# Rotary halves swapped by DMA, softmax row sums on ScalarE, and a reordered start of self-attention in a gated cross-attention and mixture-of-experts layer

## The chip, the cores and the metric

One core of a Trainium2 chip runs the whole layer in one launch. The metric is the device time in microseconds of one execution. Lower is better.

## The reference, cut to what matters

Eight sequences of 100 rows by 512 go through gated cross-attention (16 heads of 128 over 361 context rows), and the result, normalised, goes through a block with its own causal self-attention (16 heads of 32, rotary positions) and a mixture of experts. The change touches the self-attention and what feeds it:

```python
h = _rms(x, w_ln1)                       # x: the layer-normed rows after cross-attention
q, k, v = h @ wq + bq, h @ wk + bk, h @ wv + bv    # 16 heads of 32
def rot(t):
    t1, t2 = (t[..., :D // 2], t[..., D // 2:])
    return jnp.concatenate([-t2, t1], axis=-1)
q, k = q * cos + rot(q) * sin, k * cos + rot(k) * sin
scores = jnp.einsum('bqhd,bkhd->bhqk', q, k) * HEAD_DIM ** (-0.5)   # causal mask, then
attn = jax.nn.softmax(scores, axis=-1)
ctx = jnp.einsum('bhqk,bkhd->bqhd', attn, v)
```

## The kernel before, in words

**Engines and order.** Five programs, one for each of SyncE (SP, the loads of weights), ScalarE (ACT), VectorE (DVE), GpSimd (POOL) and TensorE (PE), walk the same list of steps. The list of this part is `steps_ffn` (L216 to L300). Each engine does its share of a step in the order of the list and waits on semaphores in that order; nothing is taken out of turn.

**Precision.** Most products are three matmuls of rounded high and low parts. ScalarE makes the high part, DVE (activations, L1290) or POOL (weights, L1827) subtracts it to get the low part. A weight tile costs an SP load (L731) into one of four `raw` buffers, a ScalarE copy (L846) and a POOL subtraction. Weights are loaded six units and split four units ahead of the matmuls that use them.

**Halves.** The eight sequences are two halves of four. While PE does the last projection of cross-attention, the first half is already normalised and transposed to `HTh`/`HTl`. For each sequence b of the second half the chain is: `resid` b (PE transposes `YT`; DVE adds it to `XR` and takes the statistics, L1441 and L1442), `norm1` b (DVE, `Z`), `square` b (ScalarE root), `row` b (DVE, into `HR`), `turn` b (PE transposes, ScalarE writes `HTh`, DVE `HTl`). Before the change all of it stands between `vrow` 0 and `qk` (0,1): PSUM banks 6 and 7 serve `resid`, banks 4 and 5 serve `turn`, which are free until the first softmax tile is transposed. `vrow` k (four of them) are the value projection, 12 matmuls each; its bias add (four DVE instructions, L1485) stands in `vrow` 3.

**Query and key tiles.** There are 16, (h, n) with h the half and n from 0 to 7; n even is a query tile, n odd the key tile of the same four heads. `qk` (h, n) is 12 matmuls of 400 columns into bank 6 or 7, then ScalarE writes `PQ[..][:, 0, :]` with bias (L1044). There are two `PQ` buffers; ScalarE waits that the tile two before is done. `rope` (h, n) is on DVE a shuffle of the halves of each head into `PQ[..][:, 1, :]` (L1472), a product with `sinT` (L1474) and, once POOL's product with `cosT` (L1889) is there, the sum (L1477). In the second part of the list `rope` stands right behind the `at` step beside which its tile was made.

**Self-attention.** `at` n, for n from 0 to 35, is one pipeline step; score tile u (one head of each of four sequences, 100 rows by 4 x 100) is taken through it:

- every fourth step PE makes the scores of four tiles (mask by matmul, then 16 small products; `f_scores`), after the exponentials of the four tiles before;
- in step u: DVE takes the row minimum (`f_max`, L1497), ScalarE the exponential, four instructions of 100 columns (L1066);
- in step u + 1: DVE sums the rows of the exponentials (L1519) and inverts the sum (L1520), POOL multiplies (L1897);
- in step u + 3: PE transposes (L2264), ScalarE or DVE (L1507) copies to `PTf`;
- every fourth step, `f_out`: PE multiplies with the values into bank 4, ScalarE writes `CXh`, DVE `CXl`. Bank 4 is also one of the two for transposed tiles, so the next odd tile's transposition waits for `CXl`.

Beside the steps stand matmuls that PE can do meanwhile: `qk` (0,4) to (0,7) at 0, 1, 3, 4, the values of the second half (`vbat`) at 6 to 9, `qk` (1,0) to (1,5) at 10, 11, 13, 15, 17, 18, the output projection `po` of half 0 at 20 to 23, `qk` (1,6) and (1,7) at 24 and 25, and from 24 on the epilogue of half 0 (`er`: residual and statistics on DVE; `eroot`, `erms`, `eh`: norm and transposition; router).

**Banks.** `banks` in the class `Plan` deals banks 6 and 7 alternately to the steps that use them, in the order of the list, and notes which semaphore says that the last user is done.

Of the kernel before, what the change touches and what calls it, by code (L numbers as in the profile page):

```python
# [43 lines left out]
ROUTE = {"order": 2, ("sg", 0): 5, "picks": 6, ("sg", 1): 8, "pad": 10, "eid": 11, "pos": 12, "idx": 13, "mine": 14}  # L44
SWAP = [(i + 16) % 32 for i in range(32)]

# [169 lines left out]
def steps_ffn():  # L216
# [21 lines left out]
    yield from vrow(0) + [("resid", 4), ("norm1", 4)]
    yield from vrow(1) + [("square", 4), ("row", 4), ("resid", 5), ("norm1", 5)]
    yield from vrow(2) + [("square", 5), ("row", 5), ("resid", 6), ("norm1", 6), ("turn", 4)]  # L240
    yield from vrow(3) + [("square", 6), ("row", 6), ("resid", 7), ("norm1", 7), ("turn", 5)]
    yield from qk(0, 0) + [("square", 7), ("row", 7), ("rope", 0, 0), ("turn", 6)]
    yield from qk(0, 1) + [("rope", 0, 1), ("turn", 7)]
    yield from qk(0, 2) + [("rope", 0, 2)]
    yield from qk(0, 3) + [("rope", 0, 3), ("router_split",)]
# [80 lines left out]
class Plan:  # L326
# [86 lines left out]
    def banks(self):  # L413

        empty = {6: ("dve_x1", 7), 7: ("dve_x1", 8)}
        self.bank, self.bank_free = {}, {}
# [13 lines left out]
        for s in self.ffn:  # L430
            if s[0] == "qk":
                use(s, ("act_f", s[1] * 8 + s[2] + 1))
# [45 lines left out]
def flamingo_kernel(nc, x, ctx_in, mask, g_x, g_f, Wq, Wk, Wv, Wo, w_ln1, wq, b_q, wk, b_k, wv, b_v, wo,  # L478
# [242 lines left out]
    def sync_program(eng):  # L721
# [62 lines left out]
        def zero_rows():  # L784
# [46 lines left out]
    def scalar_program(eng):  # L831
# [191 lines left out]
        def turn(b):  # L1023
            act.wait_ge(sem("pe_ht"), b + 1)
            src = banks[4 + b % 2][:, 0:KD * T].rearrange("p (k t) -> p k t", k=KD)
            eng.activation(HTh[b // HB][:, :, batch_slice(b)], src, ACT.Copy).then_inc(sem("act_ht"), 1)
# [20 lines left out]
        def self_attention(n):  # L1047
# [227 lines left out]
    def vector_program(eng):  # L1275
# [157 lines left out]
        def resid(b):  # L1433
# [4 lines left out]
            dve.wait_ge(sem("pool_const"), CONST["causal"])  # L1438
            stt(XR[:, i, :], banks[6 + i % 2][0:T, :], tgx[:, 0:1], XR[:, i, :], ALU.mult, ALU.add).then_inc(sem("dve_x1"), 1)
            dve.wait_ge(sem("dve_x1"), b + 1)  # L1440
# [21 lines left out]
        def turn(b):  # L1462
            dve.wait_ge(sem("act_ht"), b + 1)
            src = banks[4 + b % 2][:, 0:KD * T].rearrange("p (k t) -> p k t", k=KD)
# [14 lines left out]
        def v_row(k):  # L1479
            if k < KD - 1:  # L1480
                return
            for i in range(HB):
# [16 lines left out]
        def self_attention(n):  # L1499
# [245 lines left out]
        for name, *a in plan.ffn:  # L1745
# [12 lines left out]
            elif name == "rope":  # L1758
                rope(*a)
            elif name == "vrow":  # L1760
                v_row(*a)
            elif name == "vadd":
# [208 lines left out]
    def tensor_program(eng):  # L1971
# [178 lines left out]
        def resid(b):  # L2150
            half, i = divmod(b, HB)
            pe.wait_ge(sem("act_yt"), KD * (half + 1))
            if i >= 2:
                pe.wait_ge(sem("dve_x1"), b - 1)
            elif i == 0:
                pe.wait_ge(sem("dve_pt"), 2 * NS * (half + 1))
            else:
                pe.wait_ge(sem("dve_o"), NS * (half + 1))
            for f in range(KD):
                e = eng.transpose(banks[6 + i % 2][0:T, f * 128:(f + 1) * 128], YT[:, f, i * T:(i + 1) * T], ident[:, :])  # L2160
            e.then_inc(sem("pe_rows"), 1)

        def turn(b):
            if b >= 2:
                pe.wait_ge(sem("dve_ht"), b - 1)
            elif b == 0:
                pe.wait_ge(sem("dve_j"), plan.job_end[1])
            else:
                pe.wait_ge(sem("dve_pt"), 4 * NS)
            pe.wait_ge(sem("dve_row"), b + 1)  # L2170
            for k in range(KD):
                e = eng.transpose(banks[4 + b % 2][:, k * T:(k + 1) * T], HR[b % 3][:, k * 128:(k + 1) * 128], ident[0:T, 0:T])
            e.then_inc(sem("pe_ht"), 1)
# [39 lines left out]
        def f_scores(q):  # L2213
# [19 lines left out]
        def f_out(q):  # L2233
# [5 lines left out]
            if q:  # L2239
                pe.wait_ge(sem("dve_cx"), q)  # L2240
            else:
                pe.wait_ge(sem("dve_ht"), B - 1)
            for b in range(HB):
# [279 lines left out]
```

## Time and profile before

| | |
|---|---|
| runs, median of 3 | 1006.71 us (1005.0 to 1008.25) |
| profiled execution, its own time | 1002.62 us |
| its span, first to last instruction | 1000.8 us |
| mean granted TensorE clock | 0.949 |
| PE busy / DVE / ACT / POOL | 90% / 67% / 55% / 42% |

The profiled execution is 4.1 us (0.4%) below the median. The profile records every instruction with its start and length in us from the span's start; "[4.03 <-POOL PF L1897]" behind a record is the idle time of its engine ahead of it and what ended it. Matmuls are pipelined, so the length of one is more than the distance to the next. `vrow` 0 starts at 471.8 us and the last step of self-attention ends at about 655 us; the change lies wholly in between.

### The profile page before, as it was taken

The page shows a single profiled execution, that of the slowest core. Times are in us where ns is not written, and L with a number is a line of the kernel's source. Part 1 is how long each engine was busy: PE and PEld are TensorE (multiplying, and loading weights), DVE is VectorE, ACT ScalarE, POOL GpSimd, SP SyncE. Part 2 cuts the span into 40 slices and gives each one's busy share as a digit, 9 for nine tenths or more (in the row PEclk, how much of TensorE's full clock was granted, in tenths as well). Part 3 has the DMA queues.
Part 4 walks back from the last instruction along what each step waited for, and adds up shares of the span by engine and source line. Part 5 has one row for each costly group of instructions (what it writes and reads, how often), then busy time and mean ns, then how long its engine had stood idle before and what let it go on. Part 6 is the DMA issues. An engine that isn't in the chain of part 4 may idle for free.

```text
span 1000.8 us, 16056 instructions
## 1 busy us (share of the span) xinstructions
PE 903.5 (90%) x5713; PEld 838.3 (84%) x5713; DVE 666.5 (67%) x1492; ACT 555.3 (55%) x1305; POOL 422.0 (42%) x405
## 2 busy tenths in 40 slices
PE   4999999999999999999887884899887989999995
PEld 4889999999989999998676774698877988898884
DVE  4557777753747776732887758656855878897853
ACT  3656666744556666644345452435435667776750
POOL 3442322345532322346376552254272545565531
PEclk9999999999999999999989796599998999999998
DMA  5763000035520000035222120033478799999975
GB/s 141 207 229 91 1 1 2 11 98 151 155 68 16 2 1 1 12 85 142 86 64 64 38 60 21 1 97 94 161 220 218 220 292 285 295 307 292 275 181 143
DMA packets 125687, 120.75 MB, mean 121 GB/s; under 512 B 12644, under 2 KB 96556, under 8 KB 125008
## 3 DMA queue, kind: packets, MB, share of 16 engines
q1 hardware_dynamic: 106510, 96.09, 31.3%
q0 software_dynamic: 5120, 10.22, 5.1%
q10 hardware_dynamic: 13978, 13.41, 4.8%
q8 instruction: 46, 0.75, 0.3%
q14 instruction: 33, 0.27, 0.1%
HBM read 102.16 MB, written 17.53 MB: 120 GB/s over the span
## 4 chain that ended last, share of the span: by engine, by line
PE 58%; DVE 15%; DMA 13%; ACT 5%; issue 5%; POOL 4%; ACTq 0%; SPq 0%; POOLq 0%; DVEq 0%
PE bank L1976 52%; DMA eraw<-in_L_ffn_w_down_e_dram 4%; PE bank L2103 3%; DVE we L1290 2%; DMA s_sum<-yo,target 2%; POOL s_rows L1904 2%; DVE PQ L1474 1%; DMA eraw<-in_L_ffn_w_gate_e_dram 1%; ACT we L860 1%; DMA eraw<-in_L_ffn_w_up_e_dram 1%; DMA s_rows<-HR,idx 1%; DMA raw<-in_L_xattn_Wq_dram 1%; DMA sums<-s_sum 1%; DVE wf L1290 1%; DVE PQ L1472 1%
## 5 line engine op out<-in xcount | busy, mean ns | idle before, releaser
L1856 POOL TENSOR_SCALAR SC<-SC,mx,anyv 100x361 f32<-100x361 f32 x128 | 81.5, 647 | 211.3 <-DVE mx L1403 200.9
L1839 POOL TENSOR_TENSOR we<-eraw,we 128x704 fp32r<-128x704 f32 x40 | 72.7, 1818 | 112.0 <-ACT we L860 110.3
L1827 POOL TENSOR_TENSOR wx<-raw,wx 128x512 fp32r<-128x512 f32 x64 | 83.5, 1313 | 80.4 <-ACT wx L846 80.3
L860 ACT ACTIVATE we<-eraw 128x704 fp32r<-128x704 f32 (+2 forms) x140 | 96.6, 718 | 29.6 <-DMA eraw<-in_L_ffn_w_down_e_dram 16.5
L1290 DVE TENSOR_TENSOR we<-eraw,we 128x704 fp32r<-128x704 f32 (+2 forms) x100 | 92.8, 946 | 24.4 <-ACT we L860 24.1
L1976 PE MATMUL bank<-H2h,wf 128*128 128x400 f32 x352 | 102.1, 357 | 0.0
L1827 POOL TENSOR_TENSOR wf<-raw,wf 128x512 fp32r<-128x512 f32 x54 | 70.9, 1317 | 60.5 <-ACT wf L846 60.2
L975 ACT ACTIVATE SC<-SC,mx 100x361 f32<-100x361 f32 x128 | 75.4, 593 | 27.7 <-DVE mx L1399 27.1
L1976 PE MATMUL bank<-XTh,wx 128*128 128x400 f32 x256 | 72.7, 357 | 2.8 <-POOL wx L1827 1.4
L1290 DVE TENSOR_TENSOR Kl<-bank,Kh 128x362 fp32r<-128x362 f32 x64 | 34.2, 535 | 60.2 <-ACT Kh L933 60.2
L846 ACT ACTIVATE wf<-raw 128x512 fp32r<-128x512 f32 x100 | 61.8, 629 | 19.3 <-DMA raw<-in_L_ffn_w_sh_down_dram 7.6
L1290 DVE TENSOR_TENSOR QOl<-bank,QOh 128x200 fp32r<-128x200 f32 (+1 forms) x96 | 41.5, 432 | 44.4 <-ACT QOh L889 34.3
L1976 PE MATMUL bank<-QOh,wx 128*128 128x400 f32 x256 | 70.5, 347 | 0.0
L1976 PEld LDWEIGHTS bank<-H2h,wf 128*128 128x128 f32 x352 | 67.7, 194 | 0.3 <-issue 0.2
L1396 DVE CUSTOM_DVE_ANT_0 SC<-bank,mb 100x361 f32<-100x361 f32 x128 | 62.7, 528 | 0.3
L1976 PE MATMUL bank<-H2l,wf 128*128 128x400 f32 x176 | 62.0, 353 | 0.0
L966 ACT ACTIVATE PTh<-bank 128x400 fp32r<-128x400 f32 x64 | 32.3, 505 | 50.1 <-PE bank L2103 50.0
L1290 DVE TENSOR_TENSOR wf<-raw,wf 128x512 fp32r<-128x512 f32 x46 | 48.0, 1051 | 17.5 <-ACT wf L846 17.0
L1290 DVE TENSOR_TENSOR PTl<-bank,PTh 128x400 fp32r<-128x400 f32 (+1 forms) x128 | 53.3, 459 | 7.5 <-ACT PTh L966 7.5
L1066 ACT ACTIVATE PF<-bank,sm 100x100 f32<-100x100 f32 x128 | 33.7, 355 | 44.2 <-DVE sm L1497 44.2
L1897 POOL TENSOR_TENSOR PF<-PF,sm 100x400 f32<-100x400 f32 x32 | 27.9, 873 | 69.1 <-DVE sm L1520 69.1
L846 ACT ACTIVATE wx<-raw 128x512 fp32r<-128x512 f32 x64 | 40.0, 627 | 30.5 <-PE bank L1976 12.2
(265 smaller groups left out, 2824.8 us busy)
## 6 DMA issues: line engine op xcount, KB each, us to landing
eraw<-in_L_ffn_w_gate_e_dram SPq DMA_DIRECT2D x40, 352.0 KB, 3.9
eraw<-in_L_ffn_w_up_e_dram SPq DMA_DIRECT2D x40, 352.0 KB, 5.6
eraw<-in_L_ffn_w_down_e_dram SPq DMA_DIRECT2D x40, 256.0 KB, 6.3
raw<-in_L_xattn_Wq_dram SPq DMA_DIRECT2D x32, 256.0 KB, 3.1
raw<-in_L_xattn_Wo_dram SPq DMA_DIRECT2D x32, 256.0 KB, 3.0
raw<-in_L_ffn_w_sh_gate_dram SPq DMA_DIRECT2D x22, 256.0 KB, 3.4
raw<-in_L_ffn_w_sh_up_dram SPq DMA_DIRECT2D x22, 256.0 KB, 3.3
s_rows<-Z SPq DMA_DIRECT2D x6, 800.0 KB
```

The lines of the kernel that those rows point to most:

```text
L846: eng.activation(weights(stream, u)[:, 0, :, :], raw[r % 4][:, :, :], ACT.Copy).then_inc(sem("act_w"), 1)
L860: eng.activation(weights("e", u)[0:rows, 0, 0:n], eraw[u % 6][0:rows, 0:n], ACT.Copy).then_inc(sem("act_e"), 1)
L966: eng.activation(flat(PTh[t % 2][:, 0:2, :]), banks[5][:, 0:4 * T], ACT.Copy).then_inc(sem("act_pt"), 1)
L975: eng.activation(sc, sc, ACT.Exp, bias=mx[t % 3][:, 1, h:h + 1], scale=XS, accum_out=mx[t % 3][:, 2, h:h + 1]).then_inc(sem("act_exp"), 1)
L1066: e = eng.activation(p[:, c, :], bank[0:T, c * T:(c + 1) * T], ACT.Exp, bias=m[:, 1, c:c + 1], scale=-1.0)
L1290: return eng.tensor_tensor(o, src, f32(hi), ALU.subtract)
L1396: eng.tensor_tensor_reduce(SC[t % 3][:, h, :], banks[h][0:T, 0:S], mb[:, :], 1.0, -3.0e38, ALU.add, ALU.max, m[:, 0, h:h + 1]).then_inc(se ...
L1827: eng.tensor_tensor(w[:, 1, :, :], raw[plan.raw[stream, u] % 4][:, :, :], f32(w[:, 0, :, :]), ALU.subtract).then_inc(sem("pool_w"), 1)
L1839: eng.tensor_tensor(w[0:rows, 1, 0:n], eraw[u % 6][0:rows, 0:n], f32(w[0:rows, 0, 0:n]), ALU.subtract).then_inc(sem("pool_e"), 1)
L1856: eng.tensor_scalar(sc, sc, m[:, 3, h:h + 1], anyv[:, b:b + 1], ALU.mult, ALU.mult).then_inc(sem("pool_p"), 1)
L1976: return eng.matmul(o, a, b, start=start, stop=stop, skip_group_check=True)
L2103: e = eng.transpose(dst, SC[t % 3][:, h, o:o + n], ident[0:T, 0:T])
```

## The change

- **Sums**: the exponential on ScalarE also gives the sum of its row (`accum_out`); the DVE reduction L1519 goes.
- **Swap**: the shuffle L1472 goes. SP waits for `PQ[..][:, 0, :]` and issues eight DMAs of 16 partitions by 400 elements (25.6 KB each) that write each half of a head's rows to the place of the other; DVE waits for all eight. They stand in SP's program where `rope` stands in the list.
- **Order**: `norm1`, `square`, `row`, `turn` are spread later; the bias add of the values becomes a step (`vout`) ahead of `turn` 4; `qk` (0,3) goes behind the first scores, so that three tiles instead of five are made before them; each later tile of half 0 moves by one to two steps.
- **Banks**: `resid` and `turn` of the second half take banks 6 and 7 from the same deal as the `qk` tiles. First scores and first transpositions wait for `turn` 3 only.

```diff
+    yield from vrow(0) + [("resid", 4)]
+    yield from vrow(1) + [("resid", 5), ("norm1", 4), ("square", 4)]
+    yield from vrow(2) + [("resid", 6), ("row", 4), ("norm1", 5), ("square", 5)]
+    yield from vrow(3) + [("row", 5), ("vout",), ("turn", 4)]
+    yield from qk(0, 0) + [("norm1", 6), ("square", 6), ("rope", 0, 0), ("turn", 5)]
+    yield from qk(0, 1) + [("row", 6), ("rope", 0, 1), ("resid", 7), ("router_split",)]
+    yield from qk(0, 2)
...
-    beside = {0: qk(0, 4), 1: qk(0, 5), 3: qk(0, 6), 4: qk(0, 7), 6: v[0], 7: v[1], 8: v[2], 9: v[3],
+    beside = {0: [("rope", 0, 2), ("turn", 6)], 1: qk(0, 3) + [("norm1", 7), ("square", 7)], 2: [("row", 7)] + qk(0, 4),
+              3: qk(0, 5) + [("turn", 7)], 4: qk(0, 6), 5: qk(0, 7), 6: v[0], 7: v[1], 8: v[2], 9: v[3],
...
-        empty = {6: ("dve_x1", 7), 7: ("dve_x1", 8)}
+        empty = {6: ("dve_pt", 4 * NS), 7: ("dve_o", 2 * NS)}
...
+            if s[0] == "resid" and s[1] >= HB:
+                use(s, ("dve_x1", s[1] + 1))
+            elif s[0] == "turn" and s[1] >= HB:
+                use(s, ("dve_ht", s[1] + 1))
...
+        def rotate(h, n):
+            at = 8 * h + n
+            p = PQ[at % 2]
+            sp.wait_ge(sem("act_f"), at + 1)
+            for q in range(8):
+                a, b = 16 * q, 16 * (q ^ 1)
+                eng.dma_start(p[a:a + 16, 1, :], p[b:b + 16, 0, :]).then_inc(sem(f"dma_rot{at % 2}"), 16)
...
                     e = eng.activation(p[:, c, :], bank[0:T, c * T:(c + 1) * T], ACT.Exp, bias=m[:, 1, c:c + 1],
-                                       scale=-1.0)
+                                       scale=-1.0, accum_out=m[:, 2, c:c + 1])
...
         def rope(h, n):
-            dve.wait_ge(sem("act_f"), at + 1)
-            chained(eng.stream_shuffle(p[:, 1, :], p[:, 0, :], SWAP))
+            dve.wait_ge(sem(f"dma_rot{at % 2}"), 128 * (at // 2 + 1))
...
                 dve.wait_ge(sem("act_fe"), u + 1)
-                chained(eng.tensor_reduce(m[:, 2, :], PF[u % 4][:, :, :], AX, ALU.add))
                 eng.reciprocal(m[:, 3, :], m[:, 2, :]).then_inc(sem("dve_fr"), 1)
...
         def f_scores(q):
-                pe.wait_ge(sem("dve_ht"), B)
+                pe.wait_ge(sem("dve_ht"), HB)
```

## Rows read from the trace of the kernel before

**Rows 1.** Busy time by stretch: window, length, then busy (count) of each engine
```profile
core 0: us, PE busy (x) PEld busy (x) DVE busy (x) ACT busy (x) POOL busy (x), PEclk, DMA share, GB/s
471.00:505.00 34.00, 29.23 (x140) 24.18 (x140) 25.43 (x51) 12.03 (x26) 16.84 (x27) 0.90 0.35 99
...
523.00:545.00 22.00, 20.34 (x173) 15.48 (x166) 17.70 (x37) 11.20 (x37) 11.81 (x13) 1.00 0.13 39
545.00:582.00 37.00, 24.89 (x257) 21.34 (x255) 28.78 (x56) 17.70 (x55) 22.40 (x22) 0.82 0.19 58
...
600.00:622.00 22.00, 8.70 (x69) 7.91 (x68) 17.79 (x37) 6.24 (x17) 6.53 (x7) 0.72 0.08 24
```

**Rows 2.** Waits, 545 to 583 us: total, times, longest
```profile
ACT PF L1066 <- DVE sm L1497: 16.5, 6, 4.3
...
PE bank L2264 <- DVE CXl L1290: 7.0, 2, 4.8
```

**Rows 3.** The chain that ended last, 471 to 655 us, by line
```profile
by line: PE bank L1976 31.8%; DVE PQ L1474 8.0%; issue 7.9%; DVE PQ L1472 3.6%; PE bank L2264 3.3%; DVE sm L1497 3.2%; POOL wf L1827 2.9%; ACT PF L1066 2.7%; DVE HR L1287 2.6%; DVE sm L1519 2.1%; DVE KT L1477 2.1%; POOL PF L1897 2.0%; DVE Q
```

**Rows 4.** The two DVE operations that go, and the product behind the shuffle: ns min/median/max
```profile
L1472 DVE STREAM_SHUFFLE PQ<-PQ x16: 593/602/619, 497.6 to 612.2; 128x400 f32<-128x400 f32 x16
L1474 DVE TENSOR_TENSOR PQ<-PQ,sinT x16: 574/1362/3009, 498.2 to 612.9; 128x400 f32<-128x400 f32 x16
...
L1519 DVE TENSOR_REDUCE sm<-PF x32: 555/559/571, 513.7 to 646.7; 100x4 f32<-100x400 f32 x32
```

**Rows 5.** Exponentials of cross-attention, which have a sum: timeline, ScalarE
```profile
201.32 0.60 ACT L975 ACTIVATE SC<-SC,mx 100x361 f32<-100x361 f32 x1
...
201.81 0.20 ACT L975 ACTIVATION_READ_ACCUMULATOR SC<-SC,mx 100x1 f32 x1
201.90 0.59 ACT L975 ACTIVATE SC<-SC,mx 100x361 f32<-100x361 f32 x1
```

**Rows 6.** Small transfers issued back to back on ScalarE's queue: timeline
```profile
24.60 0.36 ACTq L894 DMA_DIRECT2D mask<-in_mask_BxS_bf_dram  x1
24.99 0.36 ACTq L895 DMA_DIRECT2D Z<-in_c_causal_dram  x1
```

**Rows 7.** DMA issues, 455 to 620 us: count, KB each, median us to landing
```profile
raw<-in_L_ffn_wv_dram SPq DMA_DIRECT2D x6, 256.0 KB, 2.6
...
WR<-in_L_ffn_w_sh_eg_dram ACTq DMA_DIRECT2D x1, 2.0 KB, 3.3
```

**Rows 8.** The same chain in order of time: start, us, what
```profile
451.43 6.58 PE bank L1976 x36
```

**Rows 9.** TensorE at the first scores, first transposition, second scores: timeline
```profile
505.13 0.85 PE L1976 MATMUL bank<-causb,identb 100*100 100x400 bf16 x4 [0.22 <-DVE HTl L1290]
...
515.48 0.91 PE L2264 MATMUL bank<-ident,PF 100*100 100x100 f32 x4 [4.03 <-POOL PF L1897]
...
521.51 0.85 PE L1976 MATMUL bank<-causb,identb 100*100 100x400 bf16 x4 [0.47 <-ACT PF L1066]
```

**Rows 10.** Fourth scores to fifth scores, around tile (1,2): timeline
```profile
552.44 1.54 PE L1976 MATMUL bank<-causb,identb 100*100 100x400 bf16 x4
...
559.30 0.60 ACT L1044 ACTIVATE PQ<-bank,bqn 128x400 f32<-128x400 f32 x1 [1.46 <-PE bank L1976]
...
562.46 0.56 DVE L1507 COPY PTf<-bank 100x400 f32<-100x400 f32 x1
563.08 0.89 PE L1976 MATMUL bank<-PTf,V 100*32 100x100 f32 x32 [0.56 <-DVE PTf L1507]
565.45 0.57 DVE L1290 TENSOR_TENSOR CXl<-bank,CXh 128x400 fp32r<-128x400 f32 x1 [1.27 <-ACT CXh L1058]
566.84 1.54 PE L1976 MATMUL bank<-causb,identb 100*100 100x400 bf16 x4
```

**Rows 11.** Tiles (1,6) and (1,7) on DVE: timeline
```profile
602.85 3.01 DVE L1474 TENSOR_TENSOR PQ<-PQ,sinT 128x400 f32<-128x400 f32 x1
...
612.22 0.60 DVE L1472 STREAM_SHUFFLE PQ<-PQ 128x400 f32<-128x400 f32 x1
```

More of the change, by code:

```diff
@@ L44 @@
 ROUTE = {"order": 2, ("sg", 0): 5, "picks": 6, ("sg", 1): 8, "pad": 10, "eid": 11, "pos": 12, "idx": 13, "mine": 14}
-SWAP = [(i + 16) % 32 for i in range(32)]
 WO_AT = (NS - 6, NS, NS + 1, NS + 2)
@@ L236, in qk @@
         return [fetch, ("qk", h, n)]
[L238 to L245, printed above, removed]
+    yield from vrow(0) + [("resid", 4)]
[5 more added lines that the diff above has]
+    yield from qk(0, 2)
     v = [[("vbat", 0), fetch], [("vadd", 0), ("vbat", 1), fetch], [("vadd", 1), ("vbat", 2)], [("vadd", 2), ("vbat", 3)]]
     po = [[[fetch, ("po", h, m)] for m in range(KD)] for h in range(2)]
-    beside = {0: qk(0, 4), 1: qk(0, 5), 3: qk(0, 6), 4: qk(0, 7), 6: v[0], 7: v[1], 8: v[2], 9: v[3],
+    beside = {0: [("rope", 0, 2), ("turn", 6)], 1: qk(0, 3) + [("norm1", 7), ("square", 7)], 2: [("row", 7)] + qk(0, 4),
+              3: qk(0, 5) + [("turn", 7)], 4: qk(0, 6), 5: qk(0, 7), 6: v[0], 7: v[1], 8: v[2], 9: v[3],
               10: [("vadd", 3), fetch, fetch] + qk(1, 0), 11: qk(1, 1), 13: qk(1, 2), 15: qk(1, 3), 17: qk(1, 4),
@@ L430, in banks @@
         for s in self.ffn:
-            if s[0] == "qk":
+            if s[0] == "resid" and s[1] >= HB:
+                use(s, ("dve_x1", s[1] + 1))
+            elif s[0] == "turn" and s[1] >= HB:
+                use(s, ("dve_ht", s[1] + 1))
+            elif s[0] == "qk":
                 use(s, ("act_f", s[1] * 8 + s[2] + 1))
@@ L816, in sync_program @@
                 asked["f"] += 1
+            elif name == "rope":
+                rotate(*a)
             elif name == "fetch_e":
@@ L1024, in turn @@
             act.wait_ge(sem("pe_ht"), b + 1)
-            src = banks[4 + b % 2][:, 0:KD * T].rearrange("p (k t) -> p k t", k=KD)
+            src = banks[plan.bank["turn", b] if b >= HB else 4 + b % 2][:, 0:KD * T].rearrange("p (k t) -> p k t", k=KD)
             eng.activation(HTh[b // HB][:, :, batch_slice(b)], src, ACT.Copy).then_inc(sem("act_ht"), 1)
@@ L1438, in resid @@
             dve.wait_ge(sem("pool_const"), CONST["causal"])
-            stt(XR[:, i, :], banks[6 + i % 2][0:T, :], tgx[:, 0:1], XR[:, i, :], ALU.mult, ALU.add).then_inc(sem("dve_x1"), 1)
+            bank = banks[plan.bank["resid", b] if b >= HB else 6 + i % 2]
+            stt(XR[:, i, :], bank[0:T, :], tgx[:, 0:1], XR[:, i, :], ALU.mult, ALU.add).then_inc(sem("dve_x1"), 1)
             dve.wait_ge(sem("dve_x1"), b + 1)
@@ L1463, in turn @@
             dve.wait_ge(sem("act_ht"), b + 1)
-            src = banks[4 + b % 2][:, 0:KD * T].rearrange("p (k t) -> p k t", k=KD)
+            src = banks[plan.bank["turn", b] if b >= HB else 4 + b % 2][:, 0:KD * T].rearrange("p (k t) -> p k t", k=KD)
             at = batch_slice(b)
@@ L1479, in v_row @@
         def v_row(k):
-            if k < KD - 1:
-                return
             for i in range(HB):
@@ L1759, in vector_program @@
                 rope(*a)
-            elif name == "vrow":
-                v_row(*a)
+            elif name == "vout":
+                v_row(KD - 1)
             elif name == "vadd":
@@ L2152, in resid @@
             pe.wait_ge(sem("act_yt"), KD * (half + 1))
[L2153 to L2156, printed above, removed]
-            else:
-                pe.wait_ge(sem("dve_o"), NS * (half + 1))
+            if half:
+                bank = free_bank(("resid", b))
+            else:
+                bank = banks[6 + i % 2]
+                if i >= 2:
+                    pe.wait_ge(sem("dve_x1"), b - 1)
+                elif i == 0:
+                    pe.wait_ge(sem("dve_pt"), 2 * NS)
+                else:
+                    pe.wait_ge(sem("dve_o"), NS)
             for f in range(KD):
-                e = eng.transpose(banks[6 + i % 2][0:T, f * 128:(f + 1) * 128], YT[:, f, i * T:(i + 1) * T], ident[:, :])
+                e = eng.transpose(bank[0:T, f * 128:(f + 1) * 128], YT[:, f, i * T:(i + 1) * T], ident[:, :])
             e.then_inc(sem("pe_rows"), 1)
         def turn(b):
[L2164 to L2167, printed above, removed]
-            else:
-                pe.wait_ge(sem("dve_pt"), 4 * NS)
+            if b >= HB:
+                bank = free_bank(("turn", b))
+            else:
+                bank = banks[4 + b % 2]
+                if b >= 2:
+                    pe.wait_ge(sem("dve_ht"), b - 1)
+                elif b == 0:
+                    pe.wait_ge(sem("dve_j"), plan.job_end[1])
+                else:
+                    pe.wait_ge(sem("dve_pt"), 4 * NS)
             pe.wait_ge(sem("dve_row"), b + 1)
             for k in range(KD):
-                e = eng.transpose(banks[4 + b % 2][:, k * T:(k + 1) * T], HR[b % 3][:, k * 128:(k + 1) * 128], ident[0:T, 0:T])
+                e = eng.transpose(bank[:, k * T:(k + 1) * T], HR[b % 3][:, k * 128:(k + 1) * 128], ident[0:T, 0:T])
             e.then_inc(sem("pe_ht"), 1)
@@ L2240, in f_out @@
                 pe.wait_ge(sem("dve_cx"), q)
-            else:
-                pe.wait_ge(sem("dve_ht"), B - 1)
             for b in range(HB):
@@ L2255, in self_attention @@
                     pe.wait_ge(sem("dve_v"), HB)
-                    pe.wait_ge(sem("dve_ht"), B - 1)
+                    pe.wait_ge(sem("dve_ht"), HB)
                 elif u % 2 == 0:
```

## The prediction

> **What bounds the kernel now.** I first cut the stretch of the change, 471 to 655 us, into stages by busy time [rows 1]. Up to 505 PE has 29.2 of 34 us; from 523 to 545 it has 20.3 of 22 and is the bound. From 545 to 582 it has only 24.9 of 37 at a granted clock of 0.82, while DVE has 28.8: the softmax pipeline and the tiles (1,0) to (1,5) keep DVE late, and PE waits. From 600 to 622 PE has 8.7 of 22 and DVE 17.8 (tiles (1,6), (1,7), epilogue). The waits of 545 to 583 say how [rows 2]: ScalarE waited 16.5 us for row minima, PE 7.0 us for `CXl`, both from DVE. The chain that ended last [rows 3] holds, besides matmuls (31.8% of 184 us), the sin product with 8.0%, the shuffle with 3.6% (6.6 us) and the row sum with 2.1% (3.9 us). So what counts is not DVE's total but when DVE gets through its queue, in order: a wait in it costs as much as work.
>
> **The change, part by part.**
>
> *Row sums.* Gone from DVE: 32 x 0.56 = 17.9 us busy, about 0.5 each in the pipeline [rows 4]. Added on ScalarE: one accumulator read per instruction. In cross-attention the read starts 0.49 after its exponential and the next exponential 0.09 after the read [rows 5]; so 4 x 0.09 = 0.4 us more per step, 12 us in all, on an engine busy 17.7 of 37 us in the tightest stage [rows 1]. From exponential to reciprocal the way is equal (+0.4, and -0.5 for the reduction); from exponentials to the next scores it is 0.4 longer, once in four steps. Bounds for the read: 0.09 (added distance) and 0.20 (its own length) each; I take 0.09, as four stand in a row.
>
> *Swap.* Gone: 16 shuffles of 0.60 [rows 4]. In their place, for each tile: SP waits for `PQ`, issues eight DMAs, DVE waits for the last. The distance of two issues is 0.39 [rows 6], so the eighth is issued 7 x 0.39 = 2.7 us after the first; SP spends 3.1 us a tile, 50 in all. The landing of 25 KB within SBUF is nowhere in the trace. The nearest rows are 2.6 us for 256 KB and 3.3 for 2 KB, both out of HBM [rows 7]; that the smaller is not the faster says size is not the price. Above I allow 3.3; below, 0.4 (one issue and nothing). I take 2.3, a little under the nearest row, as 25 KB is a tenth of it. Together **5.0 us** from `PQ` to sin product (3.1 to 6.0), against 0.6. So +4.4 us per tile wherever DVE stands ready and something hangs on what is queued behind `rope`: the next row minimum, then exponential, then scores; the copies to `PTf`; `CXl`.
>
> The Trainium skill, SBUF — State Buffer, section "Can I just issue two DMAs to hit both halves?", says that two transfers at different partitions serialize; this is taken up under the rivals. The skill's DMA: Bandwidth & Descriptors, section Anatomy of one DMA, puts the fixed price of a transfer at about 2.0 us (for GpSimd's path); an estimate with it is 4.7 us a tile and a total some 1.5 us lower.
>
> *POOL against DVE.* The sin product has min 0.57, median 1.36, max 3.0 us for one shape [rows 4]; it is long where POOL works beside it (3.01 at 602.85 [rows 11]). After the change it starts some 4 us later, when POOL's cosine product of the tile is over, and I take 0.57 to 0.9: this gives back about 0.8 a tile.
>
> *Start (471 to 523).* One tile is 12 matmuls at 6.58/36 = 0.18 us, 2.2 us [rows 8]. DVE order is now row 5, value bias, `turn` 4, norm 6, rope (0,0), `turn` 5. Stepping through: `vrow` 3 ends at 486, value bias at 490.9, `turn` 4 low part 491.5, so bank 7 is free for `turn` 5 only then (PE idle 2.3). rope (0,0) is fed at 495.1 and done at 497, `turn` 5 low part 497.6: `resid` 7 waits for that bank (idle 3). rope (0,1) is fed at about 500.8, `resid` 7 on DVE 503.3, `turn` 6 on PE 503.4 (idle 2 to 3), first scores 503.9. Before they were at 505.1 [rows 9], with five tiles made; now three. rope (0,2) stands ahead of the first minimum: fed at 506.8, minimum at 509.5. The idle of 4.0 us ahead of the first transposition at 515.5 [rows 9] is filled by (0,3) to (0,5). The second scores come at 521.6 against 521.5 [rows 9], but (0,7) is still to be made: **+2.0** (0 to +5).
>
> *523 to 545.* PE-bound; DVE has slack for (0,6) and (0,7), and PE's waits there are under 2 us: **0**. If the cover goes (DVE late by a rotation at 528 and 532, ahead of `f_out` 0) it costs up to 2.
>
> *545 to 582.* Three links. (a) Ahead of the fourth scores DVE already waited 3 us for POOL at tile (1,0); rotation (1,0) is fed at 549.6, so most is covered: +1.2, and +0.5 for the accumulating exponential: +1.7. (b) Fourth to fifth scores took 14.4 us [rows 10]. The chain is `PQ` written at 559.9, shuffle and products, copy to `PTf` 562.5, `f_out` 563.1, `CXl` 565.4, scores 566.8 [rows 10]. The shuffle's 0.6 becomes 5.0; exponential +0.4; less stretching -0.3; sums not on this stretch: +4.2 (rounded down for PE's overlap). (c) Fifth scores to `po`: tile (1,4) +4.1, but (1,5) is landed by the time DVE gets there: -0.6 for its shuffle, -0.8 for its product: +2.7. Sum **+8.6**.
>
> *582 to 600.* `po` keeps PE busy, no tiles: **0**.
>
> *600 to 655.* Tile (1,6): `PQ` at 599.7, fed at 604.7, done 605.9, against 606.4 (the 3.01 goes [rows 11]): -0.5. Tile (1,7): DVE waited for `PQ` [rows 11], so +4.4 - 0.3, ahead of the statistics and root of the epilogue. Behind it three sums on the chain, -1.5, and one exponential, +0.5: **+2.6**.
>
> **Sum:** 2.0 + 0 + 8.6 + 0 + 2.6 = +13.2 us. Against the profiled execution 1002.6 + 13.2 = 1015.8. That execution is 4.1 under the median, so the median would be 1019.9; I say **1019.5**, as the hand-stepping takes no slack twice. SP's loads are hidden: it loads six units ahead, and a tile's rotation holds it until 3.1 us after `PQ`; without this cover each dense tile costs about 2 us.
>
> **Rivals.**
>
> (A) *Relief wins.* If a landing is short and DVE comes late anyway, the chain loses shuffle and sum, 6.6 + 3.9 us [rows 3], keeps +1.5 for the reads: -9, 998. For it: DVE is the busiest engine in two stages [rows 1]. Against: at (1,2) DVE had waited for `PQ`, so the new wait is bare. It decides where `PQ` to product is under about 1.5 us; the eight issues alone are 2.7. Chance 0.12.
>
> (B) *A draw.* Start well filled (-3, as the idle of 4.0 goes), landing near 1, and the rest halved: within 3 us of 1006.7. Chance 0.09.
>
> (C) *Weights late too.* SP's loads stand behind rotations; ScalarE copies a weight in order ahead of `PQ`. Eight dense tiles at 2 us on top: +16, 1036; half of it 1028. For it: SP is now held by each tile. Against: six units ahead. Chance 0.12.
>
> (D) *The pieces go one after the other.* If each must land before the next moves, a tile takes 8 x 2.6 = 21 us [rows 7]; 16 more on five bare waits is +80, 1090. That is the rule of the page on SBUF named above. Against: weight loads issued 0.4 apart do not show it. Chance 0.03.
>
> (E) *The order undone by its banks.* `turn` and `resid` now share two banks with the tiles, so first scores are not earlier at all; this is half in my sum (+2) and bounded by +5; it stays inside the forecast.
>
> **How the numbers follow.** Forecast 0.64: its own range is 1008 (landing 0.4: five bare waits 1.9 shorter, -9.5, with start +0) to 1029 (landing 3.3, start +5, cover of 523 to 545 gone). Slower by over 0.3% (3 us, about what a measurement here can tell): 0.64 + 0.12 + 0.03 = 0.79; same 0.09; faster 0.12. The range of 8 in 10 cuts most of (A) and the top of (C) and all of (D): 1002 to 1031.
>
> **What would show it.** After: no STREAM_SHUFFLE, no TENSOR_REDUCE L1519; 128 accumulator reads with exponentials 0.33 apart; DVE idle ahead of the sin product for 3 to 5 us at (1,2), (1,4), (1,7), released by a DMA; that product near 0.6; fourth to fifth scores 18 to 19 us; first scores at 504. Wrong if: a rotation is fed under 3 us after `PQ`, or DVE's idle there is below 2 us; or ScalarE waits for `raw` loads in place of it (C); or PE's idle from 545 to 582 stays near 12 us.

## The result, and the profile after

The changed kernel takes 1046.92 us in the median of 4 runs (1045.45 to 1049.71), against 1006.09 for the kernel before in 4 runs: ratio 1.0406 [1.0378, 1.0435], slower. The forecast was 1019.5 with a range of 1002 to 1031. Its sign was right; its size was a third of what came, and the result lies above the range. The profiled execution took 1045.45 us (span 1043.7), 42.8 more than the one of before (1002.62), at a mean granted clock of 0.939 (0.949 before).

The page of the kernel after, busy time, share of the span and instructions of each engine:

```profile
PE 905.2 (87%) x5713; PEld 836.7 (80%) x5713; DVE 621.1 (60%) x1428; ACT 568.0 (54%) x1435; POOL 417.0 (40%) x405
```

DVE, 67% busy before, is now 60% busy, and the share of no engine rose. What was added is waiting, not work. The clock is not the cause either: in the stretch of the change (471 to 653.4 us before, 471 to 692.9 after) the granted clock is 0.80 and 0.78, and PE is busy for 140.8 and 143.2 us.

The two operations of [rows 4] are gone. What stands in place of the shuffle is shown by the view of one tile, the buffer `PQ` (columns as in [rows 4]; below them who waited, in us in total and times, and the landing of its DMAs):

```profile
L804 SPq DMA_DIRECT2D PQ<-PQ x128: 507/589/1702, 489.6 to 651.5; - x128
...
L1488 DVE TENSOR_TENSOR PQ<-PQ,sinT x16: 574/576/1599, 497.0 to 653.4; 128x400 f32<-128x400 f32 x16
...
  DMA PQ<-PQ: 78.1, 16
```

The sin product itself fell from a median of 1.36 us to 0.58, as forecast. But DVE stood idle for 78.1 us ahead of it, at all 16 tiles; the shuffles that went were 16 x 0.60 = 9.6 us. The waits from 471 to 700 us (total, times, longest) name who stands behind DVE; the last line is that of the kernel before, 471 to 655 us:

```profile
DVE PQ L1488 <- DMA PQ<-PQ: 78.1, 16, 7.8
ACT PF L1080 <- DVE sm L1509: 75.1, 18, 9.8
...
PE bank L1987 <- DVE PTf L1519: 15.4, 4, 6.2
...
PE bank L2309 <- DVE HR L1301: 14.6, 1, 14.6
...
ACT PF L1066 <- DVE sm L1497: 44.2, 17, 4.8
```

ScalarE waits for row minima for 75.1 us in place of 44.2, up to 9.8 us at a time in place of 4.8. The chain that ended last, by line, over the same stretch (cut off by the view at its end, as in [rows 3]):

```profile
by line: PE bank L1987 26.7%; SPq L804 22.4%; DMA PQ<-PQ 10.3%; issue 7.1%; ACT PF L1080 5.6%; DVE PQ L1488 3.3%; ACT PQ L1058 2.4%; DVE sm L1509 2.3%; POOL wf L1838 2.2%; DVE PTf L1519 1.9%; PE bank L2281 1.5%; ACT wf L860 1.4%; DVE sel L1
```

A third of the chain is now the swap, and about two thirds of that third is **issuing** on SP, not landing. In [rows 3] shuffle and sin product were 11.6% together.

**Where the 42.8 us lie.** The matmul that loads the mask (`causb`) marks each of the eight score groups in both traces (four of the eight of before stand in [rows 9, 10]); between marks:

| stretch | before, us | after, us | more | forecast |
|---|---|---|---|---|
| first scores | at 505.13 | at 504.93 | -0.2 | -1.2 |
| 1st to 2nd scores | 16.4 | 27.1 | +10.7 | +2.0 up to the 2nd, (0,7) still to be made |
| 2nd to 3rd | 14.5 | 20.7 | +6.2 | 0 |
| 3rd to 4th | 16.4 | 18.7 | +2.2 | +1.7 (link a) |
| 4th to 5th | 14.4 | 20.8 | +6.4 | +4.2 (link b) |
| 5th to 6th | 19.4 | 27.8 | +8.4 | +2.7 (link c) |
| 6th to 7th | 13.0 | 13.0 | 0.0 | 0 |
| 7th to 8th | 29.1 | 36.4 | +7.2 | +2.6 (to the end) |
| 8th scores to the last product with the values (653.36, 692.92) | 25.0 | 23.6 | -1.4 | |

That is +39.6; the other 3 us come later, where they may be chance: from the last product with the values to the end, all traces of this document take 343 to 355 us (347.4 before, 350.8 after). One tile followed through, (0,2), between the first and the second scores (timelines of the kernel after; a record with x8 is eight instructions in a row):

```profile
503.84 0.59 ACT L1058 ACTIVATE PQ<-bank,bqn 128x400 f32<-128x400 f32 x1 [8.80 <-DVE KT L1491]
504.46 4.93 SPq L804 DMA_DIRECT2D PQ<-PQ  x8
...
510.71 0.58 DVE L1488 TENSOR_TENSOR PQ<-PQ,sinT 128x400 f32<-128x400 f32 x1 [5.02 <-DMA PQ<-PQ]
...
512.53 0.42 PE L1987 MATMUL bank<-HTh,wf 128*128 128x400 f32 x1 [3.47 <-DVE HTl L1304]
...
512.90 0.34 ACT L1080 ACTIVATE PF<-bank,sm 100x100 f32<-100x100 f32 x1 [5.96 <-DVE sm L1509]
...
513.14 0.19 ACT L1080 ACTIVATION_READ_ACCUMULATOR PF<-bank,sm 100x1 f32 x1
513.23 0.34 ACT L1080 ACTIVATE PF<-bank,sm 100x100 f32<-100x100 f32 x1
...
515.33 1.28 ACT L1029 ACT_TABLE_LOAD   x1
...
518.18 1.28 ACT L1080 ACT_TABLE_LOAD   x1
...
524.78 0.90 PE L2191 MATMUL bank<-ident,HR 100*128 100x100 f32 x4 [6.09 <-DVE HR L1301]
```

`PQ` is written at 504.43. Eight issues take 4.93 us, (4.93 - 0.59)/7 = 0.62 from one to the next; the eighth starts at 508.8 and its piece has landed 1.9 later, when DVE starts: 6.3 us from `PQ` to product. Behind the wait, in DVE's order, stand the low part of `turn` 6 (PE idle 3.47), the first row minimum (ScalarE idle 5.96), and behind the next tile's wait row 7 (PE idle 6.09). With sums on ScalarE the exponentials start 0.33 apart (512.90, 513.23), as forecast. Two further table loads of 1.28 us each come in, since `norm1` 7 and `square` 7, which need a root, now stand between exponentials.

Around (1,2), the stretch of [rows 10]:

```profile
571.40 1.54 PE L1987 MATMUL bank<-causb,identb 100*100 100x400 bf16 x4
...
578.96 0.60 ACT L1058 ACTIVATE PQ<-bank,bqn 128x400 f32<-128x400 f32 x1
579.59 4.94 SPq L804 DMA_DIRECT2D PQ<-PQ  x8
...
585.83 0.58 DVE L1488 TENSOR_TENSOR PQ<-PQ,sinT 128x400 f32<-128x400 f32 x1 [7.06 <-DMA PQ<-PQ]
587.42 0.56 DVE L1519 COPY PTf<-bank 100x400 f32<-100x400 f32 x1
...
588.03 1.56 PE L1987 MATMUL bank<-PTf,V 100*32 100x100 f32 x32 [6.17 <-DVE PTf L1519]
...
592.18 1.54 PE L1987 MATMUL bank<-causb,identb 100*100 100x400 bf16 x4
```

From `PQ` (579.56) to product 6.3 us again, DVE idle for 7.06; the copy to `PTf`, `f_out` (PE idle 6.17) and the fifth scores hang on it exactly as the prediction's link b says: 20.8 us where it gave 18 to 19.

And the second tile of a pair waits too (timeline, the tiles (1,4) and (1,5)):

```profile
601.57 4.94 SPq L804 DMA_DIRECT2D PQ<-PQ  x8
606.55 0.58 SPq L734 DMA_DIRECT2D raw<-in_L_ffn_wk_dram  x1
607.18 4.93 SPq L804 DMA_DIRECT2D PQ<-PQ  x8
607.81 0.57 DVE L1488 TENSOR_TENSOR PQ<-PQ,sinT 128x400 f32<-128x400 f32 x1 [7.06 <-DMA PQ<-PQ]
...
613.46 0.58 DVE L1488 TENSOR_TENSOR PQ<-PQ,sinT 128x400 f32<-128x400 f32 x1 [3.41 <-DMA PQ<-PQ]
```

SP can give a tile's pieces only when it is through with those of the tile before and a weight load: the pieces of the two tiles start 5.61 us apart, so the products are 5.65 apart whatever DVE and ScalarE do. `PQ` of (1,5) is written at 604.24, and its first piece is issued 2.9 us later, at 607.18. The prediction held (1,5) to have landed by then. Over the 16 tiles, the time from `PQ` to product is 6.3 to 11.1 us, 7.2 in the mean.

### The profile page after: what moved, and what is told of

It is laid out like the page before. It is cut to its first block, busy times and chain, and to the rows that moved or that the text cites. A ratio compares the mean times of both kernels' runs of the same rounds, so it can differ in the third digit from the quotient of the medians.

```text
span 1043.7 us, 16251 instructions
## 1 busy us (share of the span) xinstructions
PE 905.2 (87%) x5713; PEld 836.7 (80%) x5713; DVE 621.1 (60%) x1428; ACT 568.0 (54%) x1435; POOL 417.0 (40%) x405
## 4 chain that ended last, share of the span: by engine, by line
PE 55%; DMA 14%; DVE 11%; ACT 6%; issue 5%; SPq 5%; POOL 3%; ACTq 0%; POOLq 0%; DVEq 0%
PE bank L1987 49%; SPq L804 5%; PE bank L2114 3%; DMA s_sum<-yo,target 3%; DMA PQ<-PQ 2%; DVE we L1304 2%; DMA eraw<-in_L_ffn_w_up_e_dram 2%; DMA eraw<-in_L_ffn_w_gate_e_dram 2%; DMA eraw<-in_L_ffn_w_down_e_dram 2%; ACT PF L1080 1%; DVE wf L1304 1%; POOL s_rows L1915 1%; ACT we L874 1%; DMA sums<-s_sum 1%; ACT wf L860 1%
## 5 line engine op out<-in xcount | busy, mean ns | idle before, releaser
L1987 PE MATMUL bank<-H2h,wf 128*128 128x400 f32 x352 | 100.0, 350 | 0.0
L1080 ACT ACTIVATE PF<-bank,sm 100x100 f32<-100x100 f32 x128 | 42.4, 352 | 75.1 <-DVE sm L1509 75.1
L1304 DVE TENSOR_TENSOR wf<-raw,wf 128x512 fp32r<-128x512 f32 x46 | 47.5, 1041 | 19.4 <-ACT wf L860 19.0
L1488 DVE TENSOR_TENSOR PQ<-PQ,sinT 128x400 f32<-128x400 f32 x16 | 10.9, 678 | 78.1 <-DMA PQ<-PQ 78.1
```

Of the source, the lines that this page charges most:

```text
L1304: return eng.tensor_tensor(o, src, f32(hi), ALU.subtract)
L1987: return eng.matmul(o, a, b, start=start, stop=stop, skip_group_check=True)
```

## The experiments

In the texts on record W is the theory that DVE, which takes its queue in order, stands still for the transfer and holds minima, copies and low parts behind it; W2 is the same with the addition that short waits are covered by slack; T and L are that a transfer in a tile's path costs by its length, whoever waits for it and wherever; O is that the new order costs a large share, S that ScalarE is late with the sums; A to E are the prediction's rivals, C (SP's issuing makes the weights late) above all. All ratios are against the kernel before, run on the same chip beside the experiment; a number of us is the ratio's, or the difference of the two medians, and the two can lie some 2 us apart.

### The parts one by one

**Sums alone** (on the kernel before):

```diff
-                                       scale=-1.0)
+                                       scale=-1.0, accum_out=m[:, 2, c:c + 1])
...
-                chained(eng.tensor_reduce(m[:, 2, :], PF[u % 4][:, :, :], AX, ALU.add))
```

> The kernel before with the row sums on ScalarE alone; shuffle, order and banks as before. Theory W (the swap's wait in DVE's queue is the cost): the sums are a small gain, -2 to -6 us, since 3.9 us of the old chain were row sums and the accumulator reads give back 0.3 us at each fourth step. Rival S (ScalarE is now late): +2 us or more.

Measured: 1002.79 us, 0.9967 [0.9936, 0.9998], 3.3 us faster by the ratio and 1.8 by the medians. In the windows of [rows 1]:

```profile
545.00:582.00 37.00, 25.12 (x260) 21.22 (x258) 24.50 (x45) 21.03 (x91) 22.90 (x23) 0.81 0.20 58
```

DVE has 24.5 us in place of 28.8, ScalarE 21.0 in place of 17.7; PE's busy time hardly moves (25.1, before 24.9). So DVE is relieved, but the trace shows no gain from it in the stretch of the change: the last product with the values comes at 653.18, before at 653.36. (This trace is of its slowest execution, 1009.6.) That the sums alone make the kernel faster is shown only just.

**Swap alone** (on the kernel before; DVE waits for the pieces in place of its shuffle):

```diff
+            sp.wait_ge(sem("act_f"), at + 1)
+            for q in range(8):
+                a, b = 16 * q, 16 * (q ^ 1)
+                eng.dma_start(p[a:a + 16, 1, :], p[b:b + 16, 0, :]).then_inc(sem(f"dma_rot{at % 2}"), 16)
...
-            chained(eng.stream_shuffle(p[:, 1, :], p[:, 0, :], SWAP))
+            dve.wait_ge(sem(f"dma_rot{at % 2}"), 128 * (at // 2 + 1))
```

> The kernel before with the swap by DMA alone. Theory W: +30 us or more (over three quarters of the 41); DVE idle 60 to 80 us ahead of the sin product, released by a DMA. Rival O (the new order costs a large share): under +25 us here.

Measured: 1045.86 us against 1004.56, 1.0447 [1.0395, 1.0499], +41.3. The swap alone costs as much as the whole change. That is W's forecast, and O is out as the main cause. Its waits from 471 to 700 us:

```profile
POOL PF L1907 <- DVE sm L1530: 100.9, 26, 11.7
ACT PF L1077 <- DVE sm L1507: 79.9, 17, 10.0
DVE PQ L1484 <- DMA PQ<-PQ: 76.4, 16, 7.6
```

**Order and banks alone** (the kernel after with the shuffle and the DVE reduction put back):

> The kernel after with the shuffle and the DVE row sums put back: only the new order and the shared banks. Theory W: -3 to +3 us. Rival O: +8 us or more, from two more loads of ScalarE's table between the first steps and from fewer tiles made ahead of the first score.

Measured: 1009.52 us, 1.0066 [1.0038, 1.0094], +5.0 by medians: between what W and what O expected. The first scores do come 7 us earlier, at 498.27, but the second at 520.45, only 1.1 earlier than in [rows 9]; and there are three table loads of 1.28 us between them where the kernel before has one:

```profile
498.27 0.84 PE L1980 MATMUL bank<-causb,identb 100*100 100x400 bf16 x4
...
499.00 1.28 ACT L1071 ACT_TABLE_LOAD   x1
504.46 1.28 ACT L1020 ACT_TABLE_LOAD   x1
507.30 1.28 ACT L1071 ACT_TABLE_LOAD   x1
520.45 0.85 PE L1980 MATMUL bank<-causb,identb 100*100 100x400 bf16 x4
```

The work that no longer stands ahead of the first scores stands behind them: second to third scores take 21.8 us in place of 14.5. From the third scores on the marks are as far apart as before.

**Order with sums** (the kernel after with the shuffle alone put back):

> The kernel after with the shuffle put back, so without the swap alone. Theory W: the 41 us go and the sums show, -2 to -8 us against the kernel before. Rival O: still +5 us or more.

Measured: 1006.12 us, 1.0014 [0.9988, 1.004], not to be told from no change, and again between W's -2 to -8 and O's +5. This kernel is the kernel after without its swap, so its marks say where the swap's us lie:

| stretch | order with sums, us | kernel after, us | the swap's share |
|---|---|---|---|
| first scores | at 497.07 | at 504.93 | +7.9 |
| 1st to 2nd | 22.2 | 27.1 | +4.9 |
| 2nd to 3rd | 17.9 | 20.7 | +2.8 |
| 3rd to 4th | 17.1 | 18.7 | +1.6 |
| 4th to 5th | 15.1 | 20.8 | +5.7 |
| 5th to 6th | 20.7 | 27.8 | +7.1 |
| 6th to 7th | 13.3 | 13.0 | -0.3 |
| 7th to 8th | 28.4 | 36.4 | +8.0 |
| 8th to the last product with the values | 22.8 | 23.6 | +0.8 |

The sum is 38.4. The -0.2 at the first scores in the table of before and after is thus no sign that the swap is free there: the new order with the sums brings them 8.1 us forward, and the swap takes 7.9 of that back. And of the +10.7 and +6.2 behind them 5.8 and 3.4 are there without any swap.

**Sums with swap** (the kernel before, with the first two edits together):

> The kernel before with sums on ScalarE and the swap by eight DMAs, in the old order with the old banks: the kernel after without its order. The parts alone were -3.3 (sums), +41 (swap), +5 (order); the kernel after is +41. If the parts add, this is +38 and the order costs +3 on top. If the order softens the waits (more steps between tiles, as it was spread for), this is +43 or more.

Measured: 1045.66 us against 1003.47, 1.0468 [1.042, 1.0515], +42.2. On top of the swap no gain from the sums shows (1.0468 and 1.0447): what they relieve is DVE's work, and DVE now waits (85.2 us for `PQ`). The whole change, with the new order and banks beside both, stands at 1.0406; the intervals overlap, so whether the order gives a little back is not shown.

### What in the swap costs

**One piece, and four pieces.** On the swap alone, the number k of pieces is 1 or 4; each piece copies partitions in place, so the halves are copied and not swapped:

```diff
-            for q in range(8):
-                a, b = 16 * q, 16 * (q ^ 1)
-                eng.dma_start(p[a:a + 16, 1, :], p[b:b + 16, 0, :]).then_inc(sem(f"dma_rot{at % 2}"), 16)
+            for q in range(k):
+                a, w = 128 // k * q, 128 // k
+                eng.dma_start(p[a:a + w, 1, :], p[a:a + w, 0, :]).then_inc(sem(f"dma_rot{at % 2}"), 16)
...
-            dve.wait_ge(sem(f"dma_rot{at % 2}"), 128 * (at // 2 + 1))
+            dve.wait_ge(sem(f"dma_rot{at % 2}"), 16 * k * (at // 2 + 1))
```

> The kernel before with the swap by DMA as ONE copy of 128 partitions in place of eight of 16; it copies each row in place, so the rotary product is made with unswapped halves. From PQ to the sin product some 2.5 us (one issue, 1.9 us to land) in place of 6.3. Theory W1 (what costs is the length of the wait in DVE's queue, on every tile): +41 x (2.5 - 0.6)/(6.3 - 0.6) = +14 us, 10 to 18. Rival W2 (short waits are covered by DVE's lateness, only what is over a threshold costs): +5 us or less. Rival T (any transfer in the path costs, by its latency at the queues): +30 or more.

> As the run with one piece, with four copies of 32 partitions, in place again (halves unswapped). Path 3 x 0.63 + 1.9 = 3.8 us. W1: +23 us (18 to 28). W2: between the one-piece run and the eight with a bend: under +15. T: +35.

Measured: one piece 1006.63 us, 1.003 [1.0, 1.006], +2.1 by medians; four pieces 1015.6 us, 1.0125 [1.008, 1.0169], +11.1. The tile `PQ` in the trace with one piece:

```profile
L801 SPq DMA_DIRECT2D PQ<-PQ x16: 470/471/515, 495.0 to 613.3; - x16
...
  DMA PQ<-PQ: 19.3, 7
```

and with four:

```profile
L801 SPq DMA_DIRECT2D PQ<-PQ x64: 507/590/596, 496.8 to 621.6; - x64
...
  DMA PQ<-PQ: 34.5, 14
```

One piece lands in 2.2 us (median), one of four in 1.9. So the path from `PQ` to product is about 2.3, 3.8 (three issues of 0.62 and a landing of 1.9) and 6.3 us for one, four and eight pieces, and the cost +2, +11 and +41. Plain W (W1 in the texts), which has the cost grow in step with the wait, expected +14 and +23 and misses both; W2 expected at most 5 and under 15, and both came. This is no straight line: 7 of 16 tiles wait for one piece, 14 for four, all for eight, and the four more pieces from four to eight cost three times what the first four do. T, at +30 and +35, falls. That the landing is the price also falls: it hardly changes, and with one issue and one landing in the path nearly nothing is lost.

**SP busy, DVE free.** On the kernel before, the shuffle kept; SP issues eight small transfers per tile that nobody on DVE waits for:

```diff
+            sp.wait_ge(sem("act_f"), at + 1)
+            if at:
+                sp.wait_ge(sem("dma_rot"), 128 * at)
+            for q in range(8):
+                a, b = 16 * q, 16 * (q ^ 1)
+                eng.dma_start(spare[a:a + 16, :], ident[b:b + 16, 0:24]).then_inc(sem("dma_rot"), 16)
```

> The kernel before, shuffle and all, and beside it SP waits for PQ and issues eight small DMAs (16 partitions, 24 elements each) of a constant into a spare tile at each rope; nobody waits for them but SP's next eight. Theory W: -1 to +2 us, SP has the time. Rival C (weights come late since SP's loads stand behind the pieces and the wait for PQ): +8 us or more.

Measured: 1016.78 us, 1.0123 [1.0079, 1.0167], +12.3. Groups of instructions on ScalarE, 480 to 660 us (busy us and mean ns; then the idle time before them and what ended it):

```profile
L860 ACT ACTIVATE wf<-raw 128x512 fp32r<-128x512 f32 x28 | 17.7, 642 | 19.9 <-DMA raw<-in_L_ffn_wv_dram 11.2 <-DMA raw<-in_L_ffn_wk_dram 7.5 <-DMA raw<-in_L_ffn_wq_dram 1.1
```

Here ScalarE waits 19.9 us for weights, where the kernel before waits 0.1. The same group in the kernel after:

```profile
L860 ACT ACTIVATE wf<-raw 128x512 fp32r<-128x512 f32 x26 | 16.5, 645 | 0.0
```

W, at -1 to +2, misses here. Rival C is a real mechanism, and this edit pays 12 us for it. The edit brings it out too strongly, since SP also waits for the eight before to land. In the changed kernel it is absent, and ScalarE waits for no weight in the run on the kernel after with `rope` later either (below), which has all 128 issues. So the issues alone do not make the weights late. What more it takes, and whether it is the slower pace of the changed kernel that gives SP its time there, no run shows.

### Moving the wait

The last group keeps every transfer and every piece and changes where in the list `rope` stands: d steps later than its tile (in the second part of the list). This moves DVE's wait, and with it the place at which SP issues the pieces and POOL makes its cosine product; the tiles made ahead of step 0 keep their place:

```diff
+    due = []
...
-                yield ("rope",) + s[1:]
+                due.append((min(n + d, 26), ("rope",) + s[1:]))
+        while due and due[0][0] <= n:
+            yield due.pop(0)[1]
```

**On sums with swap, d = 2:**

> The old order and banks, row sums on ScalarE, swap by eight DMAs, but each rope beside the steps stands two steps later in the lists (the four ahead of step 0 as before), so that DVE comes to it when the pieces are long landed. Theory W (DVE stands in its queue): most of the 41 us go, +3 to +12 remain, from the four tiles at the start. Rival L (the latency is on the way to the scores whoever waits): +25 us or more.

Measured: 1008.2 us, 1.0055 [1.0013, 1.0098]. The 42 us of the same kernel without the delay fall to 4 to 6, as W has it. Tile `PQ`:

```profile
L804 SPq DMA_DIRECT2D PQ<-PQ x128: 507/589/1746, 494.5 to 623.4; - x128
...
  DMA PQ<-PQ: 23.2, 10
```

**On the kernel after, d = 1 at the first steps (n < 6) and 2 behind them:**

> The kernel after, whole, with nothing changed but that each rope beside the steps stands later in the lists: one step later for tiles made beside steps 1 to 5, two steps later for the rest (26 at most). Same DMAs, same instructions. Theory W (DVE standing in its queue until the pieces land is what the change costs): the +41 us fall to +5 to +15, with DVE's idle ahead of the sin product down from 78 to 20 to 35 us, the rest of it at the three tiles ahead of step 0. Rival C (SP's time: 80 us of issues, weights late): +12 at least, as with the idle pieces, and ScalarE waiting for weights. Rival L (latency on the way whoever waits): +25 or more.

Measured: 1013.65 us against 1005.42, 1.0085 [1.0049, 1.0122], +8.2 to +8.5: the same 128 issues, the same landing of 1.9 us, and four fifths of the cost gone. The pieces of tile `PQ`, and the waits from 471 to 700 us:

```profile
L807 SPq DMA_DIRECT2D PQ<-PQ x128: 507/589/1603, 490.5 to 627.2; - x128
...
ACT PF L1083 <- DVE sm L1512: 38.6, 15, 5.4
DVE PQ L1491 <- DMA PQ<-PQ: 24.0, 10, 4.6
```

ScalarE's wait for minima is halved (75.1 to 38.6, below the 44.2 of before) with DVE's for the pieces (78.1 to 24.0). This is the run that decides between W and L: from `PQ` to product it takes 6.3 to 12.1 us, 8.2 in the mean, which is longer than in the kernel after (7.2), and it costs a fifth. A transfer that costs by its length would have cost no less here.

The marks say where. The third scores come at 553.5, as late as in the kernel after (552.7; with the shuffle 537.2), so the start keeps its whole loss. From there to the last product with the values it is 107.8 us, in the kernel after 140.2, with the shuffle 117.4.

**Control: sums alone with the shuffle, d = 1**, whether the delay is a gain by itself:

> The kernel before with sums on ScalarE, and the shuffle kept, but each rope beside the steps stands one step later in the lists of DVE and POOL. DVE waited for PQ a few times (1.8 us at tile (1,2)) and for POOL's cosine product (3.0 at (1,0)); one step later both are there. If these waits count: -5 to -9 us against the kernel before, 2 to 5 better than sums alone. If DVE's work is what counts: as sums alone, -3.

Measured: 1001.45 us against 1003.47, 0.9995 [0.9971, 1.0019]. By itself it is no gain that can be told, and neither expectation is met (-5 to -9, or -3). In the trace the stretch from the third scores to the last product with the values is 110.5 us, with sums alone 116.7, so some 6 of the 32 us that the run above gains there may come from the new place of `rope` itself; the rest is put down to the wait. The control has d = 1; with 2 and the shuffle nothing was run.

**Table loads.** On order with sums, `norm1` 7 and `square` 7 are put ahead of the first softmax step, so that no root stands between exponentials:

```diff
-    yield from qk(0, 2)
+    yield from qk(0, 2) + [("norm1", 7), ("square", 7)]
...
-    beside = {..., 1: qk(0, 3) + [("norm1", 7), ("square", 7)], ...
+    beside = {..., 1: qk(0, 3), ...
```

> Sums and the new order with the shuffle (no swap), but the last norm and its root stand ahead of step 0, so that ScalarE's table for the exponential is loaded once there and not three times. The same without this was +1.6 us. If the two more table loads (2 x 1.28 us, in front of the exponentials) are what the order costs: -1 to -2 us against the kernel before, some 3 us better. If the order costs by its tiles made later: +1 to +3.

Measured: 1005.39 us, 1.0018 [0.9985, 1.0051], not to be told from 1.0014 with the loads in place, though its trace has one load in that stretch and not three. No gain from the two loads shows; with these intervals one of up to about 4 us could hide, and in the two traces the last product with the values does come at 650.3 in place of 654.5. What the order costs stays open between the loads and the tiles made later.

The version to keep, if any, is the sums alone: 1002.79 us, the only one of the twelve whose interval lies below 1, and that by a hair. With so many runs one such interval is thin evidence, and the sums with `rope` one step later (0.9995) do not bear it out.

## Why the prediction was wrong

Right were the direction, the mechanism ("a wait in it costs as much as work", DVE's queue in order), link b as a chain with its members (not its length, +6.4 and not +4.2), the zero for 582 to 600, accumulating exponentials 0.33 apart, the sin product of 0.58 once POOL is off, and first scores at about 504 (503.9 forecast, 504.93 measured). The failed steps:

1. **"5.0 us from `PQ` to sin product (3.1 to 6.0)."** It was 6.3 and more. The issue distance of 0.39 was taken from loads on ScalarE's queue [rows 6]; on SP, for pieces within SBUF, it is 0.62, so seven of them are 4.3 us and not 2.7. The landing, taken as 2.3, was 1.9. Per tile the term is 1.3 us too small, above its upper bound; SP's issuing is 82.5 us in all (16 tiles of 4.93 to 6.13) and not 50, and DVE's idle at (1,2), (1,4) and (1,7) is 7.1, 7.1 and 7.8 us and not 3 to 5. For five bare waits that makes 6.5 us of the 29.6 by which the sum (+13.2) fell short of the +42.8 of the two profiled executions. The other 23 are put down to the next two steps; no run divides them further.

2. **"Five bare waits."** This is the larger part. DVE waited at all 16 tiles. Two things were not stepped through. A pair of tiles is issued by one SP: "(1,5) is landed by the time DVE gets there" leaves out that its pieces are issued only behind those of (1,4), 5.6 us later, so link c came to +8.4 and not +2.7. And the rotations that the new order puts among rows, turns and minima of the start, (0,2) to (0,7), each hold one of these (DVE idle 2.8 to 5.1 us at each): the second scores came at 532.0 where the prediction had 521.6, and of this the swap is 12.8, as with the shuffle in the same order they come at 519.2. The stretch called "PE-bound: **0**", 523 to 545, came to +6.2, of which the swap is 2.8 and the order with the sums 3.4. PE was the bound there only as long as DVE delivered in time; a cover of "under 2 us" was left for an event of 5 to 7 us.

3. **Covers were taken as kept.** Runs with one, four and eight pieces show why that matters: +2, +11, +41. The reading that fits them, and W2's forecasts of the first two, is this: as long as the wait is about as long as the slack, it costs little, and beyond it every microsecond counts. So the size of the path and the number of bare waits are not independent factors of a product: a path a quarter longer also lays bare waits that were still covered.

4. Missed: two further table loads of 1.28 us, whose price the runs do not resolve.

One figure of the rivals does not add up: D's 80 us on top of the forecast are 1099.5, and on top of the kernel before 1087, not 1090. Nothing hangs on it.

Of the rivals, A and B are out: the kernel is neither faster nor within 3 us. C's mechanism exists (+12 us with idle pieces) but is not in this kernel, where ScalarE waits 0.0 us for weights. D is out: the pieces overlap, each landing in 1.9 us while they are issued 0.62 apart. The Trainium skill, page SBUF — State Buffer, section "Can I just issue two DMAs to hit both halves?", says that two transfers serialize; what it measured is how little two in flight gain over one (+6%), and not that one must land before the next moves, as D read it. For pieces of 25 KB the trace does not show D's reading, as eight would then take eight landings, 15 us and not 6.3; whether their bytes take turns it cannot tell. E was half right: the new order and banks alone cost 5 us, though they bring the first scores 7 us forward as long as no swap holds them.

The Trainium skill, page DMA: Bandwidth & Descriptors, advises in its section Rules for kernel authors to issue a DMA early, compute, and wait late. The change does the first and not the last; the runs with the wait one or two steps later agree with it, 42 us down to 4 to 6 and 41 down to 8.5.

## What to carry to other kernels

Before an engine's own 0.6 us instruction is given to a DMA, count issues times their distance plus the landing, on the queue that will issue them, and then ask not what the engine saves but what stands behind its wait in its order; put the wait as late in the list as the data allows, and use few pieces. Count such waits at every occurrence, at the start too, where the later `rope` did not make the loss good, and at the second of a pair, since the issuing queue works one after the other. A wait is free only while shorter than the slack around it, and "another engine is the bound here" is no cover for one several times as long as that slack.

## What the hardware showed

- Eight small transfers within SBUF, issued in a row on SP, stand 0.62 us apart (0.59 each); issuing a single one of 128 partitions takes 0.47; two loads out of HBM on ScalarE's queue stood 0.39 apart [rows 6]. A weight load issued right behind such pieces takes 0.58 too (509.44), and 0.37 when it comes some microseconds later (618.46).
- A piece of 25 KB within SBUF lands 1.9 us after its issue begins (median; 1.8 to 3.6), one of 200 KB 2.2 us after (2.1 to 3.5): size hardly counts. The Trainium skill, page DMA: Bandwidth & Descriptors, section Anatomy of one DMA, has a fixed price of about 2.0 us (for GpSimd's path); the traces come close to it here on SP's.
- A table load is 1.28 us on ScalarE, and the next activation starts at its end (515.33 + 1.28, activation at 516.63).
